# Another table for the order in which the woven halves of the attention loop are issued

## The chip, the cores and the metric

The kernel runs on one NeuronCore of one Trainium2 chip. Its engines are TensorE (PE in the rows; PEld is its weight loads), VectorE (DVE), ScalarE (ACT), GpSimd (POOL) and SyncE (SP), each with its own instruction stream; they meet only in semaphores. The metric is the device time of one execution in microseconds (us), the median of three runs.

## The reference, cut to what matters

Two transformer-like layers over x of shape (8, 512, 128). The change lies in the first layer's attention, which is computed for each of the 8 batch rows apart:

```python
w = silu(conv3(x @ wA @ wB)); w = w * rsqrt(sum(w*w) + 1e-12)      # per head, d = 8, H = 16
beta = 2 * sigmoid(x @ beta_w); g = log_sigmoid(x @ g_w + g_b)
q, k = rmsnorm(x @ Wq), rmsnorm(x @ Wk)
L = tril(w @ w.T * beta, -1) + I
A = solve_triangular(L, tril(w @ k.T, -1))
S = q @ k.T - tril(q @ w.T) @ (beta * A)
logits = S * d**-0.5 + (G_i - G_j)                                  # G = cumsum(g), causal mask
o = softmax(logits) @ v @ Wo;  x = x + gate * o
```

After it come a routed expert layer, a second attention of another kind and a spiking feed-forward layer. The change does not touch them.

## The kernel before, in words

`layer0_attention` works on one batch row of 512 tokens at a time, as chunks of 16 tokens. Its work for a row is written as two halves. The **front** makes the projections, the gates and, for distances d = 1 to 15 inside a chunk, a recurrence: each distance takes a product on VectorE (L763, L769 twice), a block sum on TensorE (L1032, L1038 twice), a second product on VectorE (L782, L787 twice), a subtraction on GpSimd (L413, L419 twice), and one more product and sum (L751, L1023). The tiles of distance d are 32(16-d) columns wide, so 480 columns is d = 1 and 32 columns is d = 15. The front ends in the chunk matrices (L1046, L1051, L1062, L1067 on TensorE, 14 masked copies L800 on VectorE).

The **back** takes a finished front through the attention itself. First it rolls keys and queries over the chunks (seven steps of L1109, L1116, L1123 on TensorE, copies L828 on VectorE and L555, L559 on ScalarE). Then come 10 groups of four score banks (L1156 with L1166 or L1160 on TensorE) whose row maxima VectorE takes (L833, four per group; L839 joins them). Then 16 weighted values for short distances (L1194 on TensorE, L873 and L884 on VectorE, L439 and L446 on GpSimd; three banks, so that the product p waits for the VectorE product p-3). Last come 14 groups of scores (L1210, L1219, L1222), their exponentials on ScalarE (L606), their products with the values (L1234), and the output (L1243 to L1271, L867, L917 to L939).

The batch rows overlap by half. A first front stands alone; then a hardware loop of seven trips runs the back of row b and the front of row b+1 together; then the last back runs beside the routing. Within a trip, nothing orders the two halves but each engine's own stream, and this is fixed when the program is built: `weave` takes one piece (up to the next `yield`) of the half that the next letter of `ORDER[engine]` names, `b` or `f`, and what is left when the string ends follows half by half. An engine takes its instructions strictly in this order; a piece that waits for a semaphore holds up all that stand behind it. All engines meet at the end of a trip (`over`, then `go`).

Of the kernel before, what the change touches and what calls it, by code (L numbers as in the profile page):

```python
# [120 lines left out]
def load_small(nc, dram, w, label):  # L121

    loaded = nc.alloc_semaphore(label + "_small")
    with nc.Block() as block:

        @block.sync
        def _(sp):
# [3 lines left out]


ORDER = {
    'pe': ('bbbbbfbbbfbffbfffbbbbbbbbbbbbbfbbbbbbfbbbbfbfbbfbbbffbbffbbbbbffbbbbbffbbbbbffbbbbbbbbbbfbbbbbfbbbbb'
           'fbbbbbfbbbbbbffbffbbbffbfbbbbfbbbbbbbbbbbbffbbbbffbbbbbbbfbbbbffbbbbbbbbbbfbbbbbbbffbbbbbbbfbbbbbffb'
           'bbbbbbbbffbbbbbbbffbbbbbbbffbbbbfffffbffffbbbbbffffbfffbbbffffbbbfbbbbbbbbbfbbbbfbfbb'),
    've': ('ffbfbbbffffbbfffbfbbffffbfffbffffbffffffffffbbbbffffbbbbfffbbbbffffbbbbfbbbbfbbbbfbbbbfbbbbfbbbbffbb'
           'bbbbbfffbbbbfffffffbffffbfffbffbbbbbbbbbbbbbbbbbbbbbffffffffbbfffffffbffffffffffffffbfffffffffffffff'
           'ffffffffffffffffffffffffbbbbfbffbfffbbbfffbb'),
    'act': ('bffbfbffffbffffbfbbbbfffbfffbbbbbbbbbbbbbbbbbbbbbbbbbbbbffbbb'),  # L140
    'po': ('bbbbbbbffffffffffffffbffffbfffbbbbbbbfffffffffffffffffffffffffff'),
}


# [2494 lines left out]
```

## Time and profile before

| | us |
|---|---|
| median of three runs | 2472.5 (2460.71 to 2488.86) |
| the profiled execution, own time | 2484.16 |
| its span in the trace | 2482.4 |
| the seven trips in it (144 to 1461) | 1317 |
| TensorE busy over the span | 2089.1 (84%) |
| VectorE busy over the span | 1607.4 (65%) |

The profiled execution lies 11.7 us above the median, inside the spread of the three. The loop holds 53% of the span. The page is read from its busy times per engine; the windows then give the trips and the stages of a trip, and the timelines give the order inside a stage. The granted TensorE clock is given as a share of 2.4 GHz; it has the levels 2.4 and 1.2 GHz, so 0.90 over a window means that a fifth of it was at 1.2.

How the rows below are laid out. A row of the windows has the stretch in us from the span's start, its length, then the busy time with the number of instructions in brackets for PE, PEld, DVE, ACT and POOL, then the granted clock, the DMA engines' share and GB/s. A row of the waits has who waited for whom, the sum in us, the number of times and the longest. A row of a timeline has the start, the time that it covers, engine, line, operation, output and input with their shapes, how many instructions it merges, and in square brackets the idle time ahead of it with what ended it. A row of the page's groups has the count, then busy us and mean ns of one, then the idle time ahead and what ended most of it.

### The profile page before, as it was taken

How to read it: one execution, taken by the hardware profiler on the slowest of the kernel's cores; microseconds unless marked ns; L12 is line 12 of the kernel's file. 1: busy time of each engine (PE TensorE's matmuls, PEld its weight loads, DVE VectorE, ACT ScalarE, POOL GpSimd, SP SyncE). 2: the span in 40 equal slices, each digit the busy share in tenths (PEclk: the TensorE clock that was granted, in tenths of full speed). 3: DMA queues.
4: the chain of work that ended last, by engine and by line, in shares of the span. 5: the costliest groups of instructions: out<-in, count | busy, mean ns of one | idle time of the engine just before them, and what ended most of it. 6: DMA issues, size and time to landing. Idle time of an engine off the chain costs nothing. (4 is left out here: it accounts for less than half of the span.)

```text
span 2482.4 us, 44309 instructions
## 1 busy us (share of the span) xinstructions
PE 2089.1 (84%) x16530; PEld 1388.0 (56%) x16530; DVE 1607.4 (65%) x3446; ACT 861.3 (35%) x1690; POOL 972.2 (39%) x999
## 2 busy tenths in 40 slices
PE   3888988987988988988988989997899982678885
PEld 2563653553663563563564567766899981334443
DVE  5968568568568568568558555733533334789986
ACT  2031331331331331232232222231366643477682
POOL 1514323314323314313313315753555558875221
PEclk7898998998998998898898888877999996799997
DMA  3102002002002002003003001115222221110000
GB/s 101 35 7 81 2 8 79 2 8 80 2 8 79 2 7 80 1 3 85 1 3 85 1 14 35 34 37 192 63 71 71 72 78 40 40 32 26 5 9 13
DMA packets 136618, 98.83 MB, mean 40 GB/s; under 512 B 14754, under 2 KB 127587, under 8 KB 136291
## 3 DMA queue, kind: packets, MB, share of 16 engines
q1 hardware_dynamic: 128226, 79.21, 10.9%
q0 software_dynamic: 8192, 16.79, 2.3%
q8 instruction: 146, 2.39, 0.4%
q14 instruction: 54, 0.43, 0.1%
HBM read 36.25 MB, written 55.57 MB: 37 GB/s over the span
## 5 line engine op out<-in xcount | busy, mean ns | idle before, releaser
L606 ACT ACTIVATE a_prep<-ps 128x1536 f32<-128x1536 f32 (+1 forms) x112 | 155.7, 1391 | 390.2 <-PE ps L1219 240.5
L413 POOL TENSOR_TENSOR a_K<-a_K,a_yU 128x480 f32<-128x480 f32 (+14 forms) x120 | 83.9, 699 | 423.6 <-DVE a_yU L782 423.6
L833 DVE TENSOR_REDUCE a_mpart<-ps 128x4 f32<-128x512 f32 x320 | 198.4, 680 | 62.2 <-PE ps L1160 58.1
L419 POOL TENSOR_TENSOR a_X<-a_X,a_txy 128x480 f32<-128x480 f32 (+14 forms) x240 | 177.8, 755 | 119.1 <-DVE a_txy L787 118.4
L1759 ACT ACTIVATE b_hid<-ps,b_stage 128x128 f32<-128x128 f32 x576 | 164.8, 369 | 138.3 <-PE ps L1863 138.3
L1743 POOL COPY b_stage<-b_w 128x1028 f32 x144 | 150.6, 1046 | 127.3 <-PE ps L1872 127.3
L1038 PE MATMUL ps<-a_txy,cst 128*128 128x480 f32 (+14 forms) x480 | 174.8, 472 | 7.8 <-DVE a_txy L769 7.8
L2003 POOL DMA_INDIRECT c_got<-rows_y,packed x128 | 151.4, 1183 | 38.3 <-issue 35.5
L787 DVE TENSOR_TENSOR a_txy<-a_wf,ps 128x480 f32<-128x480 f32 (+14 forms) x240 | 97.9, 417 | 88.2 <-PE ps L1038 85.7
L1863 PE MATMUL ps<-b_hTp,b_stage 128*128 128x128 f32 x1152 | 153.6, 277 | 0.0
L1872 PE MATMUL ps<-b_stage,b_hid 128*128 128x128 f32 x1152 | 152.3, 275 | 0.3 <-ACT b_hid L1759 0.3
L1436 POOL DMA_INDIRECT rows_h<-a_tS,r_slot x112 | 110.2, 984 | 101.6 <-issue 52.0
L769 DVE TENSOR_TENSOR a_txy<-a_bw,a_X 128x480 f32<-128x480 f32 (+14 forms) x240 | 142.4, 616 | 10.3 <-POOL a_X L419 10.3
L1863 PEld LDWEIGHTS ps<-b_hTp,b_stage 128*128 128x128 f32 x1152 | 141.5, 194 | 0.0
L1872 PEld LDWEIGHTS ps<-b_stage,b_hid 128*128 128x128 f32 x1152 | 140.2, 192 | 0.5 <-ACT b_hid L1759 0.5
L192 PE MATMUL ps<-cst 128*128 128x128 f32 x792 | 125.8, 307 | 14.4 <-PEq L209 14.4
L192 PEld LDWEIGHTS ps<-cst 128*128 128x128 f32 x792 | 112.0, 214 | 32.9 <-issue 28.9
L1156 PE MATMUL ps<-a_aux_g,a_g_hotb 24*128 24x512 bf16 (+1 forms) x320 | 104.2, 429 | 28.0 <-DVE a_mpart L833 26.6
L800 DVE TENSOR_TENSOR a_mats<-ps,cst 128x512 f32<-128x512 f32 x112 | 71.1, 683 | 75.8 <-PE ps L1067 75.8
L1835 DVE COPY b_hTp<-ps 128x128 f32<-128x128 f32 x144 | 41.9, 291 | 119.5 <-PE ps L1863 103.2
L1038 PEld LDWEIGHTS ps<-a_txy,cst 128*128 128x128 f32 x480 | 83.6, 215 | 63.6 <-DVE a_txy L769 34.4
L1032 PE MATMUL ps<-a_tU,cst 128*128 128x480 f32 (+14 forms) x240 | 93.1, 473 | 21.4 <-DVE a_tU L763 20.5
(469 smaller groups left out, 4658.7 us busy)
## 6 DMA issues: line engine op xcount, KB each, us to landing
rows_h<-a_blank SPq DMA_DIRECT2D x66, 512.0 KB, 6.5
b_hrow<-rows_h SPq DMA_DIRECT2D x144, 64.0 KB, 1.8
rows_y<-b_orow SPq DMA_DIRECT2D x144, 64.0 KB, 1.5
b_w<-in_wexp SPq DMA_DIRECT2D x16, 514.0 KB, 11.0
c_got<-rows_y,packed POOLq DMA_INDIRECT x128, 2.6
out<-xs SPq DMA_DIRECT2D x8, 256.0 KB, 2.3
cst<-in_const SPq DMA_DIRECT2D x1, 1865.5 KB, 14.7
rows_h<-a_tS,r_slot POOLq DMA_INDIRECT x112
```

The costliest lines, as they stand in the source:

```text
L192: nc.tensor.matmul(out, square, square, start=True, stop=True, skip_group_check=True)
L419: nc.gpsimd.tensor_tensor(x, x, yX[:, a, 0:n].rearrange("p (c s) -> p c s", c=NC), ALU.subtract).then_inc(e_uX.sem, 1)
L606: nc.scalar.activation(Pt[:, at:at + width, :], ps[:, 4:4 + width, :], ACT.Exp).then_inc(e_exp.sem, width)
L769: nc.vector.tensor_tensor(by_chunk(tX[:, a, 0:n]), chunks(bw[:, :])[:, :, left], chunks(X2[:, a, :])[:, :, right], ALU.mult).then_inc(e_tX ...
L833: nc.vector.tensor_reduce(mpart[:, i, j, 4 * g:4 * g + 4], ps[:, 4 + n % 4, :].rearrange("p (r j) -> p r j", r=4), AX.X, ALU.max).then_inc ...
L1038: mm(ps[:, 1 + a, 0:n], con("block8"), tX[:, a, 0:n], start=True, stop=True).then_inc(e_pX.sem, 1)
L1436: nc.gpsimd.indirect_dma_start(hrows, bass.IndirectOffsetOnAxis(R.slot[:, n, k:k + 1], 0), R.htok[:, b % 2, t, :], None).then_inc(R.e_sent ...
L1743: nc.gpsimd.tensor_copy(stage[:, p % 3, :], we[:, bass.ds(e, 1), :]).then_inc(e_stage.sem, 1)
L1759: last = nc.scalar.activation(hid[:, p % 2, f, :], ps[:, p % 2, 128 * f:128 * f + 128], ACT.Gelu, bias=stage[:, p % 3, AT_B1 + f:AT_B1 + f ...
L1863: last = mm(ps[:, q % 2, 128 * f:128 * f + 128], stage[:, q % 3, 128 * f:128 * f + 128], hTp[:, q % 2, :], start=True, stop=True, skip_gro ...
L1872: last = mm(ps[:, 4 + r % 2, 0:D], hid[:, r % 2, f, :], stage[:, r % 3, F + D * f:F + D * f + D], start=f == 0, stop=f == NF - 1, skip_gro ...
L2003: nc.gpsimd.indirect_dma_start(got[:, b % 2, k, t, :], None, yrows, bass.IndirectOffsetOnAxis(R.packed[:, n, k:k + 1], 0))\
```

## The change

`ORDER`, the table for the seven trips, has other strings for all four engines. `ORDER_FIRST` and `ORDER_END` stay. Every instruction is still there; within a half they keep their order, and only how the halves interleave is another.

```diff
-    'act': ('bffbfbffffbffffbfbbbbfffbfffbbbbbbbbbbbbbbbbbbbbbbbbbbbbffbbb'),
-    'po': ('bbbbbbbffffffffffffffbffffbfffbbbbbbbfffffffffffffffffffffffffff'),
+    'act': ('bbffbfbbffbffbbfffffbbbfbfffbbfbbfbbbbbbbbbbbbbbbbbbbbbffbbbb'),
+    'po': ('bbbbbbbffffffffffffffbfffbfbbbfbbbfbffffffffffffffffffffffffffff'),
```

**Place one: the start of a trip on TensorE.** L969 to L976 are the front's transposes and projections; the rest is the back's rolling. Before:

```order
L1109 MATMUL ps<-a_roll_k,a_mats 128x128 x4
L1116 MATMUL ps<-a_roll_q,a_mats 128x128 x4
L969 MATMUL ps<-cst,a_txy 128x128 [waits a_xn]
L969 MATMUL ps<-cst,a_txy 128x128 x3
L1123 MATMUL ps<-a_mats 128x128 [waits a_vm]
L1123 MATMUL ps<-a_mats 128x128
L1088 MATMUL ps<-cst,a_Sd 128x128 [waits a_sdm]
L1088 MATMUL ps<-cst,a_Sd 128x128 x3
L973 MATMUL ps<-a_txy,s_wq 128x512 [waits a_hT]
L974 MATMUL ps<-a_txy,s_wk 128x512
L975 MATMUL ps<-a_txy,s_wv 128x512
L976 MATMUL ps<-a_txy,s_wA 32x512
L1109 MATMUL ps<-a_roll_k,a_mats 128x128 [waits a_kc]
```
And now:

```order
L1109 MATMUL ps<-a_roll_k,a_mats 128x128 x4
L1116 MATMUL ps<-a_roll_q,a_mats 128x128 x4
L1123 MATMUL ps<-a_mats 128x128 [waits a_vm]
L1123 MATMUL ps<-a_mats 128x128
L1088 MATMUL ps<-cst,a_Sd 128x128 [waits a_sdm]
L1088 MATMUL ps<-cst,a_Sd 128x128 x3
L969 MATMUL ps<-cst,a_txy 128x128 [waits a_xn]
L969 MATMUL ps<-cst,a_txy 128x128 x3
L1109 MATMUL ps<-a_roll_k,a_mats 128x128 [waits a_kc]
L1109 MATMUL ps<-a_roll_k,a_mats 128x128 x3
L1116 MATMUL ps<-a_roll_q,a_mats 128x128 [waits a_qc]
L1116 MATMUL ps<-a_roll_q,a_mats 128x128 x3
L1123 MATMUL ps<-a_turned_m,a_mats 128x128 [waits a_tm]
L1123 MATMUL ps<-a_turned_m,a_mats 128x128
L973 MATMUL ps<-a_txy,s_wq 128x512 [waits a_hT]
L974 MATMUL ps<-a_txy,s_wk 128x512
```
The front's transposes L969 have moved behind L1123 and the second L1088, and a whole rolling step more (L1109, L1116, L1123) stands between them and the projections.

**Place two: the row maxima on VectorE.** L833 are the back's maxima, all other rows the front's recurrence. Before, groups five to ten of the ten:

```order
L833 TENSOR_REDUCE a_mpart<-ps 128x4 [waits a_s] x4
L763 TENSOR_TENSOR a_tU<-a_wf,a_K 128x384 [waits a_uU]
L833 TENSOR_REDUCE a_mpart<-ps 128x4 [waits a_s] x4
L769 TENSOR_TENSOR a_txy<-a_bw,a_X 128x384 [waits a_uX]
L833 TENSOR_REDUCE a_mpart<-ps 128x4 [waits a_s] x4
L769 TENSOR_TENSOR a_txy<-a_bw,a_X 128x384 [waits a_uX]
L833 TENSOR_REDUCE a_mpart<-ps 128x4 [waits a_s] x4
L751 TENSOR_TENSOR a_tS<-a_qf,a_K 128x416 [waits a_pS]
L833 TENSOR_REDUCE a_mpart<-ps 128x4 [waits a_s] x4
L782 TENSOR_TENSOR a_yU<-a_bw,ps 128x384 [waits a_pU]
L787 TENSOR_TENSOR a_txy<-a_wf,ps 128x384 [waits a_pX]
L833 TENSOR_REDUCE a_mpart<-ps 128x4 [waits a_s] x4
```
And now, the first four groups:

```order
L833 TENSOR_REDUCE a_mpart<-ps 128x4 [waits a_s] x4
L740 TENSOR_TENSOR a_gspl<-a_yU,a_gspl 128x512 [waits a_gsp]
L763 TENSOR_TENSOR a_tU<-a_wf,a_K 128x480 [waits a_k,a_uX0]
L769 TENSOR_TENSOR a_txy<-a_bw,a_X 128x480
L833 TENSOR_REDUCE a_mpart<-ps 128x4 [waits a_s] x4
L769 TENSOR_TENSOR a_txy<-a_bw,a_X 128x480
L782 TENSOR_TENSOR a_yU<-a_bw,ps 128x480 [waits a_pU]
L787 TENSOR_TENSOR a_txy<-a_wf,ps 128x480 [waits a_pX]
L833 TENSOR_REDUCE a_mpart<-ps 128x4 [waits a_s] x4
L787 TENSOR_TENSOR a_txy<-a_wf,ps 128x480 [waits a_pX]
L763 TENSOR_TENSOR a_tU<-a_wf,a_K 128x448 [waits a_uU]
```
and the last ones:

```order
L833 TENSOR_REDUCE a_mpart<-ps 128x4 [waits a_s] x4
L782 TENSOR_TENSOR a_yU<-a_bw,ps 128x416 [waits a_pU]
L787 TENSOR_TENSOR a_txy<-a_wf,ps 128x416 [waits a_pX]
L833 TENSOR_REDUCE a_mpart<-ps 128x4 [waits a_s] x4
L787 TENSOR_TENSOR a_txy<-a_wf,ps 128x416 [waits a_pX]
L763 TENSOR_TENSOR a_tU<-a_wf,a_K 128x384 [waits a_uU]
L833 TENSOR_REDUCE a_mpart<-ps 128x4 [waits a_s] x4
L769 TENSOR_TENSOR a_txy<-a_bw,a_X 128x384 [waits a_uX]
L839 TENSOR_REDUCE a_mrow<-a_mpart 128x64 [waits a_mic,a_max]
```
The first group now comes ahead of L740 and of all of distance 1; before, it stood behind L740, the six pieces of distance 1 (L763, L769 twice, L782, L787 twice) and two of distance 2. Between two groups there are now two or three front pieces; before there were three or four between the first groups and a single one between the late ones.

**Place three: the weighted values on TensorE.** L1194 are the back's, L1032, L1038 and L1023 the front's. Before:

```order
L1194 MATMUL ps<-a_shared,cst 128x512 [waits a_pd]
L1032 MATMUL ps<-a_tU,cst 128x320 [waits a_yU,a_tU]
L1038 MATMUL ps<-a_txy,cst 128x320 [waits a_yX,a_tX]
L1194 MATMUL ps<-a_shared,cst 128x256
L1038 MATMUL ps<-a_txy,cst 128x320 [waits a_yX,a_tX]
L1194 MATMUL ps<-a_shared,cst 128x480
L1194 MATMUL ps<-a_shared,cst 128x224 [waits a_mulv]
L1194 MATMUL ps<-a_shared,cst 128x448 [waits a_mulv]
L1194 MATMUL ps<-a_shared,cst 128x192 [waits a_mulv]
L1023 MATMUL ps<-a_tS,cst 128x32x11 [waits a_tS]
L1194 MATMUL ps<-a_shared,cst 128x416 [waits a_mulv]
L1194 MATMUL ps<-a_shared,cst 128x160 [waits a_mulv]
```
And now:

```order
L1032 MATMUL ps<-a_tU,cst 128x352 [waits a_yU,a_tU]
L1194 MATMUL ps<-a_shared,cst 128x512 [waits a_pd]
L1194 MATMUL ps<-a_shared,cst 128x256
L1194 MATMUL ps<-a_shared,cst 128x480
L1194 MATMUL ps<-a_shared,cst 128x224 [waits a_mulv]
L1194 MATMUL ps<-a_shared,cst 128x448 [waits a_mulv]
L1194 MATMUL ps<-a_shared,cst 128x192 [waits a_mulv]
L1194 MATMUL ps<-a_shared,cst 128x416 [waits a_mulv]
L1194 MATMUL ps<-a_shared,cst 128x160 [waits a_mulv]
L1038 MATMUL ps<-a_txy,cst 128x352 [waits a_yX,a_tX]
L1194 MATMUL ps<-a_shared,cst 128x384 [waits a_mulv]
```
Before, distance 6 (320 columns) and the start of distance 7 (288) lay between or just behind the L1194; now there is only distance 5 (352 columns), and distance 6 has moved behind the first L1210.

## Rows read from the trace of the kernel before

**Rows 1.** windows, trips one and seven: length, busy us (count) by engine, clock, DMA
```profile
144.00:327.00 183.00, 159.25 (x1488) 94.33 (x1488) 130.69 (x253) 51.19 (x76) 56.62 (x67) 0.93 0.11 30
...
1269.00:1461.00 192.00, 168.83 (x1488) 100.52 (x1489) 130.12 (x253) 51.31 (x76) 56.62 (x67) 0.88 0.10 29
```

**Rows 2.** windows: four stages of trip one, last stage of trip seven
```profile
144.00:183.00 39.00, 33.50 (x190) 24.44 (x190) 27.99 (x45) 18.19 (x39) 11.80 (x10) 0.96 0.02 6
183.00:230.00 47.00, 39.40 (x344) 15.99 (x344) 41.18 (x68) 6.88 (x13) 12.40 (x12) 0.87 0.40 110
230.00:255.00 25.00, 19.98 (x75) 11.48 (x78) 23.06 (x49) 4.39 (x6) 18.58 (x19) 0.89 0.00 1
255.00:327.00 72.00, 66.37 (x885) 42.41 (x883) 38.47 (x94) 21.73 (x18) 13.85 (x28) 0.98 0.01 2
...
1383.00:1461.00 78.00, 73.08 (x890) 45.65 (x889) 38.71 (x95) 21.73 (x18) 14.49 (x28) 0.89 0.01 1
```

**Rows 3.** waits, all seven trips: who waited for whom, sum, times, longest
```profile
DVE a_mpart L833 <- PE ps L1160: 40.4, 42, 1.7
...
DVE a_prep L664 <- PE ps L979: 37.8, 7, 5.4
...
DVE a_roll_q L828 <- PE ps L1116: 31.3, 14, 3.4
```

**Rows 4.** timeline of VectorE, trip one, first stage, start of second
```profile
157.82 0.75 DVE L664 TENSOR_SCALAR a_prep<-ps,s_conv 128x512 f32<-128x512 f32 x1 [5.41 <-PE ps L979]
...
174.64 0.49 DVE L828 COPY a_roll_q<-ps 128x320 f32<-128x320 f32 x1 [1.82 <-PE ps L1116]
...
183.31 0.65 DVE L763 TENSOR_TENSOR a_tU<-a_wf,a_K 128x480 f32<-128x480 f32 x1
...
190.16 2.47 DVE L833 TENSOR_REDUCE a_mpart<-ps 128x4 f32<-128x512 f32 x4
```

**Rows 5.** timeline of VectorE, trip one, reductions in the second stage
```profile
188.71 1.53 DVE L769 TENSOR_TENSOR a_txy<-a_bw,a_X 128x448 f32<-128x448 f32 x1
...
207.63 2.48 DVE L833 TENSOR_REDUCE a_mpart<-ps 128x4 f32<-128x512 f32 x4 [0.72 <-PE ps L1160]
...
211.33 2.48 DVE L833 TENSOR_REDUCE a_mpart<-ps 128x4 f32<-128x512 f32 x4 [0.75 <-PE ps L1160]
...
229.59 0.70 DVE L839 TENSOR_REDUCE a_mrow<-a_mpart 128x64 f32<-128x320 f32 x1
```

**Rows 6.** timeline of TensorE, trip one: rolling, reduction groups, first L1210
```profile
175.78 1.06 PE L1116 MATMUL ps<-a_roll_q,a_mats 128*128 128x128 f32 x8
...
202.05 1.59 PE L1166 MATMUL ps<-a_shared,a_roll_q 32*112 32x64 f32 x56
...
210.17 1.24 PE L1160 MATMUL ps<-a_shared,a_roll_q 32*128 32x512 f32 x8
...
213.87 2.31 PE L1160 MATMUL ps<-a_shared,a_roll_q 32*128 32x512 f32 x8
...
254.58 0.39 PE L1210 MATMUL ps<-a_aux_g,a_aux_l 32*128 32x512 bf16 x3
```

**Rows 7.** timeline of TensorE, trip one, front pieces and last product
```profile
239.33 0.81 PE L1032 MATMUL ps<-a_tU,cst 128*128 128x320 f32 x2 [0.38 <-DVE a_tU L763]
...
253.43 0.73 PE L1032 MATMUL ps<-a_tU,cst 128*128 128x288 f32 x2
...
323.40 1.16 PE L1271 MATMUL ps<-s_wo,a_prep 128*128 128x128 f32 x8 [0.68 <-ACT a_prep L609]
```

**Rows 8.** timeline of GpSimd, trip one, its masks and its sums
```profile
229.66 4.99 POOL L434 TENSOR_SCALAR a_shared<-a_roll_q,cst 128x384 f32<-128x384 f32 x4 [1.32 <-DVE a_mpart L833]
...
248.73 6.34 POOL L446 TENSOR_TENSOR a_prep<-a_prep 128x448 f32<-128x448 f32 x6 [1.26 <-DVE a_prep L873]
```

**Rows 9.** the page, costliest groups: x count, busy, mean ns, idle before
```profile
L769 DVE TENSOR_TENSOR a_txy<-a_bw,a_X 128x480 f32<-128x480 f32 (+14 forms) x240 | 142.4, 616 | 10.3 <-POOL a_X L419 10.3
...
L800 DVE TENSOR_TENSOR a_mats<-ps,cst 128x512 f32<-128x512 f32 x112 | 71.1, 683 | 75.8 <-PE ps L1067 75.8
```

More of the change, by code:

```diff
@@ L133 @@
 ORDER = {
[L134 to L139, printed above, removed]
-    'act': ('bffbfbffffbffffbfbbbbfffbfffbbbbbbbbbbbbbbbbbbbbbbbbbbbbffbbb'),
-    'po': ('bbbbbbbffffffffffffffbffffbfffbbbbbbbfffffffffffffffffffffffffff'),
+    'pe': ('bbbbbbbbfbbbfbbfbfbbbbfffbbbbbbbbbbfbbbbbbbfffbbbbbbbbbbbffbbbbbfbbbbbbffbbbbffbbbbbbbbbbbfbbfbbffbb'
+           'bbbbbbbbffbffbbfbbbbbbbbbfbbbfbbbfbbbbbbbbfffbbbbbbbffbbbbffbbfbbbbbbbbffbbbbbbffbbbbfffbfbbfbbfbbff'
+           'bbfbfffbbbbfbfbffbbbbbffffbbbffbbbbffbbffffbbbbbffbfbbbbbbbfbbbbbbbfbbbbbbbbbfbbbbfbb'),
+    've': ('fbfbfbbbbffbfffffbbfbffffbbffffffffbbbbfffbbbbfffbbbbfffbbbbffbbbbffbbbbffbbfbbffbbbbffbbbbffbbbbfbf'
+           'bfbbbfbfbfffffbbfbbbbbbbbfbbbbbbbbbfbbbfbfffbffffffffbfbfffffffbffffffffffffffffffffffffffffffffffff'
+           'fffbfffffffffffffffffffffffffbbbbbfbbbbfffbb'),
+    'act': ('bbffbfbbffbffbbfffffbbbfbfffbbfbbfbbbbbbbbbbbbbbbbbbbbbffbbbb'),
+    'po': ('bbbbbbbffffffffffffbfffbfbbbfbbbfbffffffffffffffffffffffffffffff'),
 }
```

## The prediction, made before the changed kernel ran

> **What bounds the kernel now.** I read the windows first, then the waits, then the timelines of one trip. The windows of the trips [rows 1] show what a trip is made of: TensorE is busy for 159 of 183 us in trip one and for 169 of 192 in trip seven, VectorE for 130 in both. The two trips do the same work; the difference of 9.6 us in TensorE's busy time is its clock, granted at 0.93 and at 0.88.
>
> Cut by stages [rows 2], a trip has two regimes. From 144 to 183 (rolling and projections) both engines are busy most of the time and wait for each other. From 183 to 255 (row maxima, then weighted values) VectorE is busy for 41.2 of 47 and 23.1 of 25 us, and TensorE has room: 7.6 and 5.0 us idle. From 255 on (the 14 groups of scores) TensorE is busy for 66.4 of 72 us and VectorE for 38.5. So VectorE sets the pace up to the first L1210, and TensorE behind it. An order can win in two ways: fill VectorE's idle time ahead of the first L1210, or move work so that neither regime gets it on its critical engine for nothing.
>
> The waits [rows 3] say where VectorE's idle time is: 40.4 us for the scores L1160 before a group of maxima (5.8 a trip), 37.8 for L979 before L664 (5.4 a trip), 31.3 for L1116 before the copies L828 (4.5 a trip). In the timeline [rows 5] a late reduction group starts 3.70 us after the one before (207.63, 211.33), of which 2.48 are the four maxima and 0.7 is idle: between them VectorE has only one front piece, and TensorE needs its 1.24 us of L1160 [rows 6] after the last bank is free.
>
> **The change, stage by stage, for trip one.** No instruction is added or removed, and GpSimd's and ScalarE's contents stay. I lay the new order over the old durations.
>
> *First stage, up to the first group of maxima.* L664 waits for the front's projections. These now stand behind one more rolling step on TensorE; such a step is L1109 and L1116 at 1.06 and L1123 at about 0.6 [rows 6], 2.3 us as they overlap, and some of it lies beside ScalarE's work between transposes and projections. I put L664 2.0 us later. VectorE's wait of 5.41 there [rows 4] is partly filled, since one L828 and the reduction L819 have moved ahead of L664; the reciprocals behind it start 0.4 later. Later, two copies L828 stand back to back, and the second waits for its L1116: about 2.3 us, against 1.82 before [rows 4], and L710 behind it waits for ScalarE a little. The front's chain reaches its L740 1.7 us late (bounds: 0, if the wait at L828 is only moved; 3.3, if the whole step shows and a second wait of 1 us adds). But the first group of maxima no longer waits for distance 1: it starts at about 184.4, where it started at 190.16 [rows 4].
>
> *Second stage, the ten groups.* A group costs VectorE 2.48. The time to the next is that plus the front pieces between, or TensorE's round if that is longer: 3.70 with L1160 (measured), and 0.35 more with L1166 (1.59 against 1.24 us, [rows 6]), so 4.05. The new order puts three pieces of 0.62 [rows 9] between the first groups: 4.4, 4.4, 4.4. Then two pieces, 1.2 us, which are just the round: 3.8, 3.7, 3.7, then 4.3 where a group is split, then 3.7, 3.7. To the first part I add 0.9 for one L769 that runs beside a GpSimd sum, as the one of 1.53 us does [rows 5] against a mean of 0.62 [rows 9]. Sum 37.0. With the last group's 2.5 and the 0.6 of the L769 before it L839 starts at 184.4 + 40.1 = 224.5; it started at 229.59 [rows 5]. **Term: -5.1 us**, the first stage's loss within. If all rounds are minimal, it is -7; if two groups fall into a spell of 1.2 GHz, where L1160 takes 2.31 instead of 1.24 [rows 6], and one more front piece is held up by 0.9, it is -2.
>
> *Third stage, from L839 to the first L1210.* It was 229.6 to 254.6 [rows 5, 6], with VectorE at its limit. I count the front's pieces on VectorE in it: 19 before (one of distance 4, all of 5 and 6, four of 7), 13 now (the end of distances 3 and 4, all of 5, one of 6). Six fewer at 0.62 [rows 9] is -3.7. GpSimd's masks L434, 5.0 us [rows 8], now stand ahead of the distance 4 subtraction; they begin when the maxima end, and the VectorE pieces of distance 4 cover them. GpSimd's sums L446, about 1.06 each [rows 8], are now mixed with L419 but stay ahead of VectorE by a slot. L1032 of distance 5 stands right ahead of the first L1194, so this waits for its L763: +0.4. **Term: -3.3** (bounds: -3.7, and 0 if the chain through the three banks of L1194 is the limit and not VectorE's load).
>
> *Fourth stage, from the first L1210 to the end.* TensorE's front pieces that have moved behind the first L1210 are L1023 of 352 columns, L1032 and both L1038 of 320, and L1032 and one L1038 of 288: six, at 0.81 and 0.73 [rows 7], less 0.1 by which pieces overlap. All of it is on the bounding engine: **+3.9** (7.8 at 1.2 GHz is the far bound). Before, 9 distances and 12 groups of scores lay between the first L1210 and the front's end, now it is 10 and 11; the stage's 66.4 us of TensorE [rows 2] over 14 groups and 9 distances are 2.9 for one of either, and I take them as equal, so the front ends at the same point of TensorE's stream, and three groups of the back stay behind it to cover the copies L800. I cost the rest at nothing; what hides it is TensorE's stream, full at 66.4 of 72 us.
>
> **The sum.** -5.1 - 3.3 + 3.9 = -4.5 us a trip. The seven trips have the same order, so -31.5. From the profiled execution's own 2484.2 us that gives 2452.7; this execution lies 11.7 above the median of the runs, so the median comes to **2441 us** (-1.3%). The bounds by term, -7 to -2, -3.7 to 0, +3.5 to +5.5 (I take no whole trip at 1.2 GHz), add up to -7 and +3.5 a trip at worst; all worst ends together in every trip is not likely, and I take -8 to +1.5 a trip with the clock.
>
> **A rule that speaks against this.** TensorE's last stage runs at 0.98 of full clock in trip one and at 0.89 in trip seven, where it is busy for 73.1 instead of 66.4 us [rows 2]; the second stage, with the idle time in it, has 0.87. The Trainium skill, "TensorE: Matmul & The Clock Gate", section "Part 1: The HAM clock gate (the "warmup" mystery)", says that half rate is the default and that activity releases it. By this rule thinning the third stage on TensorE, where front pieces leave, invites a slow spell there and at the start of the next; the row shows 0.89 for that stage already [rows 2], so the trace neither confirms nor excludes more. It is the second rival.
>
> **The rivals.**
> 1. *Forecast*: the terms hold, -3 to -6 a trip: 2430 to 2452. Chance 0.45; 0.05 more that it is better still.
> 2. *The clock takes it back.* If TensorE idles differently, all trips could be like trip seven: busy for 168.8, against a mean of 164 between it and trip one's 159.2 [rows 1], so +4.5 a trip, which cancels the gain: 2472. For it: trips of one execution differ by 9 us for nothing else. Against it: the last stage is as full as before. Chance 0.15.
> 3. *The order's gain is eaten by waits that a walk over old durations does not see*: the strict streams of four engines meet at other places, VectorE's pieces beside GpSimd's (1.53 for 0.62), L867 behind L1234 in the fourth stage. Half of them in the third stage make -3.3 into 0 and the second's -5.1 into -3.5: +0.4 a trip, 2475. Chance 0.27.
> 4. *Slower: the front ends too late in the fourth stage.* The four sets of chunk matrices are a strict ping-pong: TensorE's next set waits for up to four copies L800 at 0.68 [rows 9], 2.7 us. Three groups of the back now cover three such waits. If the front, 1.5 distances behind where it was at the first L1210, ends after them, TensorE idles for up to 3 x 2.7 = 8.2 us a trip: -4.5 + 8.2 = +3.7, so 2498. It decides once the front's end comes more than two groups, 5.8 us, late. Against it: TensorE's stream puts L1046 ahead of three L1210 groups, and each distance in the last stage has more TensorE work beside it than its chain needs. Chance 0.08.
>
> **How the numbers follow.** A measurement of this kernel can tell about 1% (25 us) from no change; its three runs lie 28 us apart. Faster by over 1% is below 2448: case 1 and its better tail, less what of it lies above 2448 (0.08), and a little of case 3: 0.45. Slower by over 1% is above 2497: half of case 4 and the sum of cases 2 and 3 in a bad draw: 0.08. The rest, 0.47, is within. The predicted time is case 1's. The range takes in cases 2 and 3 up to 2484 and goes down to 2415, which is -8 a trip.
>
> **What would show it.** In the trace after: the first L833 of a trip about 6 us sooner relative to L763 of 448 columns; L839 about 80 us after the trip's start instead of 85; VectorE's wait for L1160 down from 40 us to under 12 in all; L839 to first L1210 at 21.5 us instead of 25.0; first L1210 to L1271 at 73 instead of 69 in a trip at full clock. VectorE's wait for L1116 stays near 31 or rises. Wrong would be: waits of TensorE for L800 in the last stage beyond 2 us a trip (case 4), a granted clock below 0.88 in most trips (case 2), or L1194 waiting for L873 for longer than before (case 3).

## The result, and the profile after

The kernel after takes 2441.6 us (median; 2438.3 to 2452.1), the kernel before, timed beside it, 2475.1 us (2460.7 to 2488.9): a ratio of 0.988, 95% interval 0.985 to 0.991. 2441 us were predicted. All ratios here compare fast executions alone, which leaves out two of the ten of p3_after_tensor_early, its profiled one among them, and three of the thirty-one of the kernel before that were timed beside it. The span of the profiled execution is 2450.3 us (before 2482.4), and the seven trips go from 144 to 1433 us: 1289 us instead of 1317, so 28 of the 32 us lie in the loop.

Windows of the kernel after: trips one, four and seven, then the four stages of trip one. Columns as in [rows 1] and [rows 2], which they answer.

```profile
144.00:330.00 186.00, 168.25 (x1487) 99.79 (x1488) 128.40 (x254) 51.04 (x76) 57.66 (x68) 0.87 0.11 30
...
699.00:879.00 180.00, 161.62 (x1487) 96.26 (x1488) 128.13 (x253) 50.95 (x76) 57.30 (x67) 0.92 0.11 31
...
1248.00:1433.00 185.00, 164.90 (x1488) 96.95 (x1490) 127.32 (x253) 50.78 (x76) 57.14 (x68) 0.89 0.11 30
...
144.00:187.00 43.00, 38.48 (x242) 28.27 (x247) 27.92 (x44) 22.36 (x48) 11.79 (x10) 0.84 0.02 6
187.00:231.00 44.00, 37.45 (x293) 14.60 (x293) 37.97 (x64) 2.56 (x4) 10.71 (x10) 0.80 0.42 116
231.00:252.00 21.00, 18.45 (x72) 11.45 (x74) 19.38 (x42) 4.28 (x6) 18.09 (x18) 0.85 0.00 1
252.00:330.00 78.00, 73.87 (x897) 45.48 (x891) 43.14 (x106) 21.84 (x18) 17.07 (x31) 0.93 0.01 2
```

The first surprise is in the first row: trip one, which the prediction walked through, is 186 us long, 3 us longer than before. It has a clock of 0.87 where [rows 1] has 0.93. Trip four, at 0.92, takes 180. The gain shows only in the mean over seven trips. So trips are compared as means from here on. A trip is cut at the start of L651, and its stages at the first L833, at L839, at the first L1210 and at the first L1271:

| mean of seven trips, us | before | after |
|---|---|---|
| start to L664 | 14.3 | 16.2 |
| start to first L833 | 47.6 | 42.5 |
| first L833 to L839 | 40.3 | 42.1 |
| L839 to first L1210 | 25.4 | 21.6 |
| first L1210 to L1271 | 71.0 | 74.3 |
| whole trip (shortest to longest) | 188.1 (182.6 to 192.3) | 184.1 (179.9 to 185.5) |
| TensorE busy in it | 164.8 | 164.6 |
| TensorE idle in it | 23.3 | 19.5 |

The last two lines are the plainest account of the gain: TensorE is busy as long as before, and its idle time fell by 3.8 us a trip. By stages the idle time went from 6.1 to 5.2, 6.5 to 6.5, 5.1 to 4.0 and 3.0 to 1.3 us; the 2.5 us behind L1271 are the same in both.

That the busy time is equal is a balance of two changes. The trace says which stretches were granted 1.2 GHz. Take off half of the busy time in them, and what is left is the work at full clock: 148.4 us a trip before and 146.4 after. The half taken off is what the slow clock cost: 16.4 us before, 18.2 after. So in these two executions the clock took back about 2 us a trip. The ends of matmuls are modelled in a profile, and why the work at full clock should fall by 2.0 us is not shown; 1.0 of it is at L1194, which had waited for L873 before.

Waits of the kernel after, all seven trips: VectorE's, which answer [rows 3], and TensorE's.

```profile
DVE a_prep L664 <- PE ps L979: 28.4, 7, 4.1
DVE a_roll_q L828 <- PE ps L1116: 26.8, 14, 2.1
...
DVE a_mpart L833 <- PE ps L1160: 19.1, 35, 2.1
DVE a_txy L660 <- ACT a_rstd L481: 11.2, 7, 1.6
DVE a_wf L710 <- ACT a_prep L532: 10.9, 7, 1.6
DVE a_mpart L833 <- PE ps L1166: 10.8, 13, 1.0
```

```profile
PE ps L1156 <- DVE a_mpart L833: 36.5, 121, 1.0
...
PE ps L1130 <- ACT a_turned_m L559: 15.0, 7, 2.2
...
PE ps L1210 <- DVE a_prep L873: 9.9, 7, 1.4
...
PE ps L1101 <- DVE a_mpart L824: 3.5, 7, 0.5
...
PE ps L1194 <- DVE a_prep L873: 1.9, 7, 0.3
```

TensorE's waits in the kernel before:

```profile
PE ps L1156 <- DVE a_mpart L833: 26.3, 107, 0.8
...
PE ps L1173 <- DVE a_mrow L839: 22.3, 7, 3.2
PE ps L1194 <- DVE a_prep L873: 18.1, 14, 1.8
PE ps L1101 <- DVE a_mpart L824: 14.4, 7, 2.1
...
PE ps L1062 <- DVE a_mats L800: 7.6, 14, 0.7
```

VectorE's waits for L1160 halved, from 40.4 to 19.1, and L1166 took up 10.8. TensorE in turn waits longer for VectorE's maxima, 36.5 us instead of 26.3 at L1156, so its idle time in the second stage is what it was. It no longer waits for L800 at L1062, hardly for L873 at L1194, not at L1173 for L839, and 1.6 us a trip less for L824 at L1101. New are its wait for ScalarE's L559, 2.1 us a trip, and 1.4 a trip at the first L1210 for L873.

The timeline of VectorE in trip one after, first and second stage, answers [rows 4] and [rows 5]:

```profile
160.60 0.75 DVE L664 TENSOR_SCALAR a_prep<-ps,s_conv 128x512 f32<-128x512 f32 x1 [4.06 <-PE ps L979]
...
176.89 0.63 DVE L828 COPY a_roll_q<-ps 128x448 f32<-128x448 f32 x1 [2.11 <-PE ps L1116]
...
179.08 0.69 DVE L710 TENSOR_TENSOR a_wf<-a_prep 128x512 f32<-128x512 f32 x1 [1.56 <-ACT a_prep L532]
...
183.71 0.69 DVE L725 TENSOR_TENSOR a_txy<-a_wf,ps 128x512 f32<-128x512 f32 x1 [1.07 <-PE ps L1001]
...
187.34 2.48 DVE L833 TENSOR_REDUCE a_mpart<-ps 128x4 f32<-128x512 f32 x4 [0.47 <-PE ps L1166]
...
201.32 1.54 DVE L769 TENSOR_TENSOR a_txy<-a_bw,a_X 128x448 f32<-128x448 f32 x1
...
220.25 2.48 DVE L833 TENSOR_REDUCE a_mpart<-ps 128x4 f32<-128x512 f32 x4 [2.14 <-PE ps L1160]
```

Four waits in a row, 2.11, 1.56, 1.07 and 0.47, stand ahead of the first group, which starts at 187.34. A group in the second stage still waits 2.14 us where a spell of 1.2 GHz meets it.

### The profile page after: what moved, and what is told of

It is laid out like the page before. It is cut to its first block and busy times, and to the rows that moved or that the text cites. A ratio compares the mean times of both kernels' runs of the same rounds, so it can differ in the third digit from the quotient of the medians.

```text
span 2450.3 us, 44308 instructions
## 1 busy us (share of the span) xinstructions
PE 2086.4 (85%) x16522; PEld 1385.6 (57%) x16530; DVE 1590.8 (65%) x3446; ACT 857.6 (35%) x1690; POOL 972.0 (40%) x999
## 5 line engine op out<-in xcount | busy, mean ns | idle before, releaser
L606 ACT ACTIVATE a_prep<-ps 128x1536 f32<-128x1536 f32 (+1 forms) x112 | 155.7, 1390 | 435.3 <-PE ps L1219 243.1
L833 DVE TENSOR_REDUCE a_mpart<-ps 128x4 f32<-128x512 f32 x320 | 199.4, 683 | 52.3 <-PE ps L1160 36.5
L1038 PE MATMUL ps<-a_txy,cst 128*128 128x480 f32 (+14 forms) x480 | 174.5, 466 | 11.2 <-DVE a_txy L769 10.8
L769 DVE TENSOR_TENSOR a_txy<-a_bw,a_X 128x480 f32<-128x480 f32 (+14 forms) x240 | 135.2, 585 | 4.3 <-POOL a_X L419 4.3
L800 DVE TENSOR_TENSOR a_mats<-ps,cst 128x512 f32<-128x512 f32 x112 | 70.6, 684 | 96.9 <-PE ps L1067 96.5
L787 DVE TENSOR_TENSOR a_txy<-a_wf,ps 128x480 f32<-128x480 f32 (+14 forms) x240 | 99.1, 419 | 48.0 <-PE ps L1038 47.2
L1156 PE MATMUL ps<-a_aux_g,a_g_hotb 24*128 24x512 bf16 (+1 forms) x320 | 98.2, 422 | 37.1 <-DVE a_mpart L833 36.7
L1038 PEld LDWEIGHTS ps<-a_txy,cst 128*128 128x128 f32 x480 | 84.8, 211 | 71.9 <-DVE a_txy L769 36.2
L1234 PE MATMUL ps<-a_prep,a_values 128*32 128x128 f32 x2560 | 118.5, 300 | 4.2 <-ACT a_prep L606 4.2
L1032 PE MATMUL ps<-a_tU,cst 128*128 128x480 f32 (+14 forms) x240 | 102.5, 514 | 22.2 <-DVE a_tU L763 22.1
```

The costliest lines, as they stand in the source:

```text
L606: nc.scalar.activation(Pt[:, at:at + width, :], ps[:, 4:4 + width, :], ACT.Exp).then_inc(e_exp.sem, width)
L769: nc.vector.tensor_tensor(by_chunk(tX[:, a, 0:n]), chunks(bw[:, :])[:, :, left], chunks(X2[:, a, :])[:, :, right], ALU.mult).then_inc(e_tX ...
L833: nc.vector.tensor_reduce(mpart[:, i, j, 4 * g:4 * g + 4], ps[:, 4 + n % 4, :].rearrange("p (r j) -> p r j", r=4), AX.X, ALU.max).then_inc ...
L1038: mm(ps[:, 1 + a, 0:n], con("block8"), tX[:, a, 0:n], start=True, stop=True).then_inc(e_pX.sem, 1)
L1234: last = mm(ps[32 * r:32 * r + 32, 7, 128 * g:128 * g + 128], vflat[:, v0:v0 + 32], Pt[:, at, 128 * r:128 * r + 128], start=j == i and g = ...
```

## The experiments

These ran on four other chips: the h kernels and after_again on one, the d and p kernels on a second, the c kernels on a third, the m kernels on a fourth. The kernel before takes 2569 to 2574 us on each; its loop is not slower there (the kernel after has 1285.4 us of loop against 1289.0), the 90 us lie behind it. Ratios are to the kernel before, timed beside each. "Busy" and "idle" are TensorE's, per trip, from the windows of the seven trips of one profiled execution; they carry the clock of that one execution, busy time most, so times are compared by the ratios. The kernel after was timed on two chips, 0.988 and 0.985, and not beside the d, p, c and m kernels. So what an edit of it costs is given as a range from both.

| | ratio (95%) | loop, us | busy | idle |
|---|---|---|---|---|
| before, first chip | 1 | 1316.8 | 164.8 | 23.3 |
| after_again | 0.985 (0.981 to 0.988) | 1285.4 | 164.0 | 19.6 |
| h1_new_then_old | 0.994 (0.991 to 0.996) | 1307.3 | 163.1 | 23.7 |
| h2_old_then_new | 0.991 (0.988 to 0.994) | 1292.4 | 164.0 | 20.6 |
| m1_new_fourth_stage | 1.015 (1.012 to 1.018) | 1361.6 | 169.8 | 24.7 |
| m2_old_fourth_stage | 0.990 (0.986 to 0.994) | 1286.6 | 161.0 | 22.8 |
| d1_before_vector_add | 1.002 (0.998 to 1.007) | 1324.9 | 166.2 | 23.1 |
| d2_after_vector_add | 0.990 (0.986 to 0.993) | 1293.5 | 164.3 | 20.5 |
| p3_after_tensor_early | 0.991 (0.987 to 0.995) | | | |
| p4_after_tensor_late | 0.996 (0.993 to 1.000) | 1307.8 | 167.9 | 19.0 |
| h3_early_front | 0.988 (0.985 to 0.992) | 1287.2 | 164.1 | 19.8 |
| c1_old_start_plain | 0.987 (0.983 to 0.991) | 1282.2 | 162.6 | 20.6 |
| c2_old_start | 0.987 (0.983 to 0.991) | 1290.3 | 163.9 | 20.5 |

> The kernel after itself, beside the three others on the same chip: 2441, ratio 0.988. It is the yardstick for the three.

Its ratio is 0.985, and the interval takes in the 0.988 expected. The time itself, 2539 us, is that of a slower chip.

**Which half of the order brings the gain?** Two kernels cut both tables at the end of the ten groups and join them crosswise.

```
h1: ORDER[e] = new[e][:cut] + what new[e][:cut] leaves of old[e]   # pe 111, ve 97, act 40, po 18
h2: ORDER[e] = old[e][:cut] + what old[e][:cut] leaves of new[e]   # pe 112, ve 102, act 40, po 22
```

> The table of after up to the end of the ten groups of maxima, behind it the table of before. VectorE comes to the cut with five front pieces fewer than in the kernel before, and makes them up right behind it: 5 x 0.62 = 3.1 us on the engine that bounds the third stage. If the two gains of the change hang together (the pieces that the second stage leaves undone must be left to the fourth), L839 comes 3.4 us sooner as in the kernel after, the first L1210 at 107.0 + 3.1 + 3.9 us, and the trip is 0 to 0.5 us shorter than before: 2472 to 2476. If the waits for L1160 that are gone were the whole gain, it keeps 3.4 us a trip: 2451.

> The table of before up to the end of the maxima, behind it the table of after. The second stage stays as long as before. The third has 8 front pieces on VectorE where before had 19: 11 x 0.62 = 6.8 us less, but the chain of L1194, L873 and GpSimd's masks can't be shorter than VectorE's own back work there, so -4 to -5 us; the fourth gets the six TensorE pieces that after has there, +3.9 to +4.2. In sum -1 to 0 us a trip: 2468 to 2475. The rival, by which filling the fourth stage costs TensorE nothing new because it had idle time for L800 and L873, gives -3 us a trip or more: 2454 or less.

Both expectations missed by their sizes. The first half of the order alone brings 0.6% in the times, 2.4 us a trip, and 9.5 us in the profiled loop, 1.4 a trip: more than the 0 to 0.5 expected. But TensorE's idle time is 23.7 us, as before. The first L1210 comes 114.0 us into the trip, just where it was expected and 0.6 later than before; the whole gain of this trace is in the fourth stage, 69.1 us instead of 71.0 for the same work at a higher granted clock. L839 came 0.7 us sooner than before, not 3.4. The 3.4 us a trip of the waits that went would be 0.991, at the very edge of the interval. The second half alone brings 0.9%, and 24.4 us in the loop, 3.5 a trip, not 0 to 1. Its stages: 45.6 to the first L833, 39.5, 18.1 and 77.6 us. The third fell by 7.3 (11 front pieces less, at 0.62, are 6.8), more than the 4 to 5 that I allowed: the chain of L1194 and L873 is no limit at 18 us. Its idle time, 2.8 us below that of before, is the larger part of its 3.5; the rest is the clock.

**Is the fourth stage paying or gaining?** The same with the cut at the first L1210.

```
m1: old[e][:cut] + rest of new[e]   # pe 141, ve 150, act 40, po all old
m2: new[e][:cut] + rest of old[e]   # pe 137, ve 139, act 40, po all new
```

> The table of before up to the first L1210, behind it the table of after: only the order within the fourth stage is new, and no front piece is deferred into it. If the fourth stage has a gain of its own (L1062 no longer waits for the copies L800, because the front's end now stands further ahead of the trip's end), TensorE's idle time in it falls from 3.2 to 1.3 us and the trip gains about 2 us, half of the change: ratio 0.992 to 0.996. The rival is the account in my prediction, by which the fourth stage only pays for what the others leave to it: then nothing is left out and nothing gained, 0.999 to 1.002.

> The table of after up to the first L1210, behind it the table of before: six TensorE pieces of the front (L1032, L1038 twice, L1023 of 320 columns, L1032 and one L1038 of 288) stand in a row ahead of the first L1210, about 4 us. If what counts is TensorE's idle time in the whole trip (23.3 us before, 19.6 after), it keeps the part that stages one and three gave, about 2 us a trip, and loses the fourth's: ratio 0.991 to 0.996. By my prediction's account it would keep 5.1 + 3.3 - 4 us, 4.4 a trip: 0.987.

Both theories missed m1: it is 1.5% slower than before. Windows of m1: trip four, its fourth stage (843 to 923), and three stretches in it.

```profile
732.00:927.00 195.00, 169.59 (x1487) 99.39 (x1488) 129.95 (x254) 51.28 (x76) 57.18 (x68) 0.88 0.10 28
843.00:923.00 80.00, 77.23 (x884) 46.98 (x881) 35.63 (x91) 21.73 (x18) 14.41 (x28) 0.83 0.01 1
844.00:860.00 16.00, 14.37 (x134) 8.19 (x134) 3.00 (x5) 4.35 (x3) 1.06 (x2) 0.50 0.00 1
860.00:888.00 28.00, 28.00 (x351) 16.90 (x351) 17.67 (x48) 8.71 (x6) 11.35 (x20) 0.98 0.01 2
893.00:902.00 9.00, 9.00 (x65) 5.42 (x67) 1.43 (x5) 3.16 (x4) 0.80 (x3) 0.51 0.01 2
```

The same stage of the kernel before, in its trip three, and of h1 in trip four:

```profile
627.00:696.00 69.00, 65.80 (x883) 42.09 (x881) 37.00 (x92) 21.73 (x18) 14.03 (x28) 0.98 0.01 2
```

```profile
817.00:884.00 67.00, 63.93 (x880) 40.70 (x877) 36.67 (x91) 21.59 (x18) 14.05 (x28) 1.00 0.01 2
```

It is the same work: busy time by clock is 77.23 x 0.83 = 64.1, 65.80 x 0.98 = 64.5 and 63.93. The idle time is 3 us in all three. The 13 us between 67 and 80 are the clock's alone: m1 runs for 16 us at 1.2 GHz from 844 on and for 9 more at 893, and four of its seven trips have this stage at 80.3 us.

Its waits say what the new order of this stage does by itself. The wait of L1062 for L800 is gone, 1.1 us a trip. But the idle time of the stage is 2.9 us, not the 1.3 that I expected, for a new wait stands in its place:

```profile
PE ps L1210 <- ACT a_prep L606: 11.4, 7, 1.6
```

It stands ahead of the second L1210, where the kernel after has front pieces of TensorE to do, and no such wait. So the order of the fourth stage takes idle time away only together with the pieces deferred into it.

m2 has the fourth stage at 68.9 us, as the quicker trips of before have it (68.8), and pays at its head: 27.0 us from L839 to the first L1210 instead of 21.6. Its ratio, 0.990 (0.986 to 0.994), is a little better than expected and keeps two thirds or more of the gain. Its interval takes in the 0.987 of my prediction's account as well, so the times alone decide nothing between the two. That its profiled execution comes out at 183.8 us a trip, as the kernel after does, is again the clock: 0.98 in this stage in every trip, against 0.93. Its idle time, 22.8, is nearer to before (23.3) than the 21.5 that its expectation implies.

The idle times of all kernels fall into place by two differences. Every kernel that defers front pieces beyond the first L1210 (after, h2, d2, p4, h3, c1, c2) has 1.3 us of idle time in the fourth stage and 3.5 to 4.5 in the third; those that don't (before, d1, h1, m1, m2) have 2.9 to 3.2 and 4.7 to 6.2. And with the new first stage TensorE idles 5.0 to 5.3 us in it, with the old one 6.0 to 6.4 (h3, in between, 5.7). Together that is 2.8 and 0.9 of the 3.8 us; h1 has the 0.9 too, but loses it again in the stages behind.

**Was VectorE's idle time between the late groups real?** One more reduction behind five of the ten groups, in both kernels (it repeats work on constants, and its result is used nowhere):

```diff
+                    if over_front and n in (19, 23, 27, 31, 35):
+                        nc.vector.tensor_reduce(junk[:, (n - 19) // 4:(n - 15) // 4], cst[:, 0:512], AX.X, ALU.max)
```

> The kernel before with one more reduction of 128x512 on VectorE (0.6 us, its result goes nowhere) behind each of five of the ten groups of maxima in a trip. By the theory of the change VectorE idles 0.7 us between the late groups here, because TensorE needs 1.24 us for L1160: the added work falls into it where it stands behind a late group, and shows where it stands behind an early one. 0 to 1 us a trip: +0 to +7 us, 2475 to 2482. The rival, by which VectorE has no room there, gives 5 x 0.62 = 3.1 us a trip: 2497.

> The kernel after with the same five reductions. VectorE's idle time between groups is filled there, so they show nearly in full: 2 to 3.1 us a trip, +14 to +22 us over the kernel after, 2456 to 2463. If they cost as little as in the kernel before (under 1 us a trip), the second stage's gain was not filled idle time, and my account of it is wrong.

VectorE in d1, trip five, two late groups (L838 is the added line; L834, L770 and L1163 are L833, L769 and L1160):

```profile
969.86 2.48 DVE L834 TENSOR_REDUCE a_mpart<-ps 128x4 f32<-128x512 f32 x4 [0.95 <-PE ps L1163]
972.26 0.68 DVE L838 TENSOR_REDUCE a_junk<-cst 128x1 f32<-128x512 f32 x1
972.85 0.55 DVE L770 TENSOR_TENSOR a_txy<-a_bw,a_X 128x384 f32<-128x384 f32 x1
973.56 2.48 DVE L834 TENSOR_REDUCE a_mpart<-ps 128x4 f32<-128x512 f32 x4 [0.16 <-PE ps L1163]
...
977.26 2.48 DVE L834 TENSOR_REDUCE a_mpart<-ps 128x4 f32<-128x512 f32 x4 [0.16 <-PE ps L1163]
```

The added 0.68 us fits into the gap: the groups stay 3.70 apart (973.56, 977.26), as in [rows 5], and the idle time shrinks from 0.72 to 0.16. The stage from the first L833 to L839 is 40.3 us with and without it. In the times d1 costs 0.002, 6 us, as expected and not to be told from nothing, while the rival's 3.1 us a trip (1.0085) lies outside its interval. d2 costs 0.002 to 0.005 over the kernel after, 0.7 to 2.0 us a trip: at or below the low end of what was expected. Its trace shows 1.0 us a trip in that stage (43.1 against 42.1) and 0.9 more idle time. VectorE's waits at L833 fall from 4.3 us a trip to 2.6, so they take up 1.7 of the added 3.4, where in d1 they fall by 3.1 and take nearly all. So the gap was there, and after fills only part of it. The loop of d1 is 8.1 us longer than that of before; that is TensorE's busy time (1.4 us a trip), at a lower granted clock, since idle time did not change.

**Where does more TensorE work cost?** L1032 and L1038 of two distances are issued twice (the same sums again).

```diff
+                    if over_back and d in (4, 5):      # p4: (6, 7)
+                        mm(ps[:, 0, 0:n], con("block8"), tU[:, 0:n], start=True, stop=True)
```

> The kernel after with L1032 and L1038 of distances 4 and 5 issued twice in the trips (384 and 352 columns), about 4.5 us more of TensorE a trip in stages two and three. If TensorE has room there it costs 0 to 1.5 us a trip: 2441 to 2452. The rival, by which the whole trip hangs on TensorE's sum of work, gives +4.5 us a trip: 2473.

> The kernel after with L1032 and L1038 of distances 6 and 7 issued twice in the trips, about 4.1 us more of TensorE a trip behind or around the first L1210. The stage is bound by TensorE, so all of it shows: +4.1 us a trip, 2470. If it costs under 2 us a trip, the term of +3.9 in my sum was no cost of moved work but something else.

p4, trip seven and its fourth stage, at full clock, and the fourth stage of h3 in its trip one, also at full clock and without the added work:

```profile
1273.00:1454.00 181.00, 161.90 (x1502) 96.73 (x1503) 127.61 (x253) 50.79 (x76) 57.33 (x68) 0.92 0.11 30
...
1377.00:1450.00 73.00, 71.61 (x904) 44.88 (x904) 41.15 (x103) 21.44 (x18) 17.29 (x31) 1.00 0.01 2
```

```profile
250.80:320.60 69.80, 68.52 (x892) 42.54 (x892) 41.50 (x103) 21.69 (x18) 16.91 (x31) 1.00 0.01 2
```

In the trace the late work shows in full: the stage holds 71.2 us of work at full clock where after has 68.1 (mean of seven), its idle time stays at 1.3, and it is 3.1 to 3.3 us longer. The added matmuls make 3.1 us a trip, not the 4.1 that I priced. In the times p4 costs 0.008 to 0.012 over the kernel after, 3.0 to 4.3 us a trip. The early work costs 0.003 to 0.0065, 1.1 to 2.4 a trip: partly above the 0 to 1.5 expected, and below the rival's 4.5. On their common chip the medians of p3 and p4 lie 8 us apart, about 1 us a trip, and their intervals overlap. The direction is the forecast's, that work ahead of the first L1210 costs less than behind it, but these runs do not show it clear of noise.

**Is there more in the first stage?** h3 brings L969 to L976 back one rolling step; c2 and c1 take the whole first stage of before, and L763 and the first L769 ahead of the first group.

```
h3, first letters:  pe  bbbbbbbbfbbbf -> bbbbbfbbbfbbb
                    ve  fbfbf -> ffbfb       act  bbffbf -> bffbbf
c1: ve  old[:34] + 'ffff' + rest of new;  pe  old[:45] + rest of new;  act  old[:38] + rest of new
c2: ve  old[:34] + 'ffff' + 'bbbb' + 'f' + 'bbbb' + 'ff' + rest of new;  else as c1
```

> The kernel after, but the start of a trip as before: the front's transposes, projections and L660, L664 stand where the old table has them (the same pieces, one rolling step ahead). L664 comes 1.9 us sooner again. If that delay is passed on to the first group of maxima and to all behind it, the trip is 1.5 to 2 us shorter than after: 2428 to 2431. The rival: the first group is held by the two copies L828 back to back and by L710 that waits for ScalarE's L532, not by L664; then it is as after within 0.3 us a trip, 2440 to 2444.

> The kernel after, with the first stage of a trip from the table of before on all four engines (the front's projections one rolling step earlier again, ScalarE's L532 ahead of its L549), and VectorE's L763 and the first L769 of distance 1 ahead of the first group of maxima instead of behind it; from the second group on as after. Theory: the first stage is held in after by what stands behind the late projections (VectorE waits for L532, TensorE for L559 and VectorE for L1001), and TensorE's idle time there is the part that can still be had. L664 at 13.3 us of the trip instead of 16.2, first L833 at about 41.5 instead of 42.4 with two or three front pieces more done, so L839 about 2 to 3 us sooner, the trip 1.5 to 3 us shorter than in after: seven trips 1265 to 1277 us against 1285 to 1289, ratio to before 0.975 to 0.982. Rival: the first stage gives nothing, because what VectorE does sooner only waits for TensorE's rolling steps, or the granted clock gives it away; then it is as after, 0.985 to 0.988.

> As the one before, but with no front piece between the first two groups of maxima (the second L769 of distance 1 stands behind the second group). The second group then waits for TensorE's scores, about 0.6 us a trip, and nothing else changes: 0 to +4 us in all against it.

h3 gained nothing, but it doesn't test what it was made for: L664 comes at 16.7 us, not at 14.3, since it waits for L979 and the edit left that behind its rolling step. VectorE's wait moved to the copies:

```profile
DVE a_roll_q L828 <- PE ps L1116: 63.4, 20, 5.8
...
DVE a_wf L710 <- ACT a_prep L532: 10.9, 7, 1.6
...
DVE a_prep L664 <- PE ps L979: 2.9, 7, 0.4
```

c1 and c2 do bring L664 to 13.8 and 13.9 us, and the new waits for L559 and L532 are gone. Yet the first group comes at 42.0 and 43.0 us, and both measure 0.987: the forecast for c2, 0.975 to 0.982, failed and its rival held. VectorE now waits for TensorE's L1166 (31.3 us in c1 instead of 10.8), and TensorE again for VectorE's L824 at L1101 (16.2 us in c1 instead of 3.5), which is where the 0.9 us of idle time come back. c1 was expected 0 to 4 us above c2; it came 1.6 below, which is no difference. No version here is measurably faster than the kernel after.

## Why the prediction was right, and where its steps were not

The figure was right within 1 us. The fall of the medians is 33.5 us where 31.5 was said, since the kernel before, timed again, came out 2.6 us higher. The mean of the second stage's term lies within its bounds, that of the third 0.1 and that of the fourth 0.3 us beside them:

- **First stage.** L664 came 2.0 us later, as said; the first L833 5.1 sooner in the mean (5.8 said). In trip one itself it came at 187.34, not 184.4: the waits for L532, L1001 and L1166, 3.1 us together, were put at "a little".
- **Second stage.** The term was -5.1 at L839; in the mean it is -3.4 (84.5 against 87.9), inside its -7 to -2. From the first group to L839 it takes 42.1 us, where 40.1 was said. The L769 beside a GpSimd sum is there, at 1.54 us as costed; the waits for L1160 fell to 19.1, not under 12. In trip one L839 came 1.3 us later than before, not 5.1 sooner, because this stage ran at 0.80 there, and at 0.87 before. In trip four of after, at 0.95, it takes 39.2 us; in trip one 43.5.
- **Third stage.** -3.8, against -3.3 and a bound of -3.7. The bound was drawn from VectorE's six pieces, and it held within 0.1. h2, 18.1 us with fewer pieces still, shows that the chain of L1194 is no limit and that VectorE's load is priced rightly (-7.3 for 11 pieces at 0.62). L1194 did not wait longer for L873, but 1.9 us in all instead of 18.1.
- **Fourth stage.** +3.2 in the mean against +3.9, and below its bound of +3.5. The prediction's six pieces, added up by its own figures, are 4.1 and not 3.9. The moved work is about that: work at full clock 63.6 before (64.0 in m2) and 68.1 after, +4.1 to +4.5. But 1.7 us of idle time went with it, and this term the prediction put at nothing. TensorE doesn't wait for L800 any more (7.6 us in the loop before, none after), nor for L606 at L1210 (5.8 before, against a new 4.2 at L1234). At full clock the stage is 67.4 us in h1 and 69.8 in h3, only 2.4 longer; the rest of the 3.2 is the clock. Rival 4 had this the wrong way round: the last sum of the recurrence, L1023, ends 25.0 us ahead of L1271 instead of 20.6, so the front's end doesn't stay at the same point of TensorE's stream, but comes sooner, and the ping-pong is covered better.
- **The sum.** -4.0 a trip against -4.5 (-4.3 with the pieces added up rightly); the part outside the loop, 4 us, makes up for it. Nothing in the change explains those 4 us.

Of its signs, the third stage came as said, 21.6 us. L839 came at 84.5 us, not about 80. The fourth stage at full clock was to be 73 us and is 69.8. VectorE's wait for L1116 was to stay near 31 or rise, and fell to 26.8.

What the runs bear out of the account by regimes is less than it claimed. d1 shows VectorE's gap, and p4 that work behind the first L1210 shows in full; that work ahead of it is cheaper is not shown. The waits that VectorE lost in the second stage take no idle time from TensorE by themselves (h1: 23.7). The trip is TensorE's busy time plus its idle time, and the order gains by what it takes from the idle time: 2.8 us where front pieces are spread over the fourth stage, and 0.9 in the first.

Rival 2, the clock, was given 0.15 as a chance that all trips become like trip seven. That didn't happen: busy time 164.6 against 164.8. (The prediction's own figures for it, 168.8 against a mean of 164, give +4.8 and not +4.5.) Nor did a slow spell come into the thinned third stage: its granted clock is 0.85 in the mean of seven trips, before and after. But in size the clock outweighs what the order does to the idle time. It made m1 slower than before with the same work and 1.4 us more of idle time, and the profiled m2 as fast as after with 3.3 more. That 2441 was met within 1 us is thus in part luck: a swing of the clock of 2 us a trip is 14 us, and the 1.7 us that the second stage gained less than said were made up by 0.5 in the third stage, 0.7 in the fourth and the 4 us outside the loop.

## What to carry to other kernels

Where one engine is busy for nearly 90% of a loop, add up its busy and idle time over all trips before giving a gain to a stage; a walk through one trip compares two states of the clock as much as two orders. Price moved TensorE work at full clock (+3.9 said, +4.1 to +4.5 measured), and look for the idle time that it covers where it lands, too. A gap that another engine sets can be tested by a dummy instruction of its size; that it is free doesn't yet mean that filling it shortens the loop.

## What the runs showed of the hardware

TensorE's clock falls to 1.2 GHz inside stretches in which the profile shows it busy without a break, and in a pattern that repeats from trip to trip. In h2, trip three, first the trip, then its fourth stage, then 14 us of it:

```profile
513.00:697.00 184.00, 163.71 (x1487) 96.92 (x1488) 128.55 (x253) 51.21 (x76) 56.15 (x67) 0.91 0.11 30
616.00:694.00 78.00, 76.70 (x895) 46.65 (x896) 41.52 (x103) 21.86 (x18) 17.00 (x31) 0.89 0.01 1
660.00:674.00 14.00, 14.00 (x101) 7.04 (x100) 2.24 (x10) 6.15 (x6) 1.13 (x4) 0.56 0.00 1
```

All seven trips of h2 have this stage within 0.1 us of 77.6, and six are 184.2 to 184.4 us long; TensorE is busy for all of the 14 us. In m1 the spell at 844 follows a wait of 1.02 us and has one of 1.63 in it, while the one at 893 follows more than 28 us without a pause. The Trainium skill, "TensorE: Matmul & The Clock Gate", section "Part 1: The HAM clock gate (the "warmup" mystery)", says that activity releases the clock; these rows show that being busy, as the profile reckons it, isn't enough. What starts such a spell stays open here: nothing was run that changes it alone, and the order of narrow and wide matmuls changes it together with all else. Its cost is not small: half of TensorE's busy time in the stretches granted 1.2 GHz is 14.5 us a trip in m2, 16.4 in before, 18.2 in after and 20.7 in m1. m2 and m1 hold the same instructions in another order, and differ in this by 6.2 us, more than the 3.8 us of idle time that the change removed. Whether an order can be chosen by it was not tried.
